# Cross attention: probabilities and keys turned by transposing DMAs in f16 parts, in place of TensorE transposes

## The chip, the cores and the metric

The kernel runs on one core of one Trainium2 chip. The metric is the device time of one execution in microseconds; lower is better. An engine has its own queue of instructions and works in order; engines wait for each other through semaphores. PE is TensorE, DVE is VectorE, ACT is ScalarE, POOL is GpSimd, SP is SyncE, which here only issues DMAs.

## The reference

Two layers on x (128 sequences x 64 positions x 128 channels) and a context of the same shape. The change is in the second layer's cross attention:

```python
x = layer_norm(image_embeds, ln1_g, ln1_b)      # the context
l = layer_norm(latents, ln2_g, ln2_b)           # the running x
q = l @ Wq
kv = concatenate([x, l], axis=1) @ Wkv          # 128 keys per sequence
q, k, v = to_heads(q), to_heads(k), to_heads(v) # 16 heads of 64
w = softmax(einsum('bhqd,bhkd->bhqk', q * scale, k * scale))
out = einsum('bhqk,bhkd->bhqd', w, v)           # heads joined, then @ Wo
```

Before it come an attention by correlation and a quantised feed-forward layer, after it a mixture of 8 experts (two per token). The expert choice of a group of four tiles (normalise, logits, top two, ranks, scatter of the rows to HBM) is computed inside the same block as this attention.

## The kernel before, in words

`build` runs three parts: `load_weights`, `first_layer`, and `attend_and_route`, which calls `cross_attention`, `apply_experts` and `combine`. Only `cross_attention` (from line 901) changes.

The weights are fused ahead: Wq with Wk per head (`qk_fused`), Wv with Wo per head (`vo_fused`), so that each head works on the 128 channels of the normalised rows themselves. Precision is kept by splitting a tensor into a high part in f16 and the rest in f16; `parts_product` (line 110) multiplies two such pairs with three matmuls, on lines 112 to 114, so these lines stand for all split products.

A tile is 128 rows, two sequences; there are 64 tiles, and 4 chunks a tile, 256 in all. A chunk is 8 heads of one sequence. Each engine walks the same steps, from -15 to 298, with one Python function `step` per engine: at step n it does stage S of chunk n + AT_S. The constants on line 976 are thus the schedule, written by hand: a stage with a larger number is done earlier. `number(i, k, off, limit)` gives the chunk and its place, `tile(i, k, off)` the tile in every fourth step, `group` the routing group in every sixteenth. Steps 64 to 239 are a loop of 16 steps, the rest is written out.

The stages of a chunk v, in order:

- tile: SP loads the rows (line 1006 context, 1007 x) to `c_rows`. DVE takes statistics (1113 to 1116), POOL the reciprocal root (1022 to 1026), DVE normalises (1123), POOL applies gain and shift and splits into f16 parts `c_kv_parts` (1030 to 1038). PE transposes the four blocks of parts (1269), and ACT copies them from PSUM to `c_kvT` (1206), of which there are two.
- G (n + 6): PE multiplies the queries' part by the fused weights, ACT writes the high part (1201), DVE the rest (1096).
- S (n + 3): PE makes the scores of 8 heads, 128x512 in PSUM; DVE takes the negated maximum of each row (1081); ACT takes the exponential, four times 128x128 with a running sum (1227), into `c_p`, f32.
- PN (n + 2): DVE inverts the sums (1091), then POOL multiplies `c_p` by them in place (1016).
- PT (n + 0): PE transposes the normalised probabilities, f32, in four matmuls into the bank `PT` (1297); ACT copies the high part to `c_pT..high` (1211), DVE subtracts it from the bank for the rest (1102). There are two such pairs.
- O (n - 1): PE multiplies the turned probabilities by the rows into the one bank `OB` (1303), ACT and DVE split it (1220, 1108).
- W (n - 5): PE sums the 16 heads with the fused weights into `WB`; X3 (n - 9): DVE adds that to x (1077).

Within a step DVE's order is: addition to x, maximum, routing's logits, reciprocal (1091), rest of G (1096), rest of PT (1102), rest of O (1108), statistics, normalising, the rest of routing. ACT's is G, keys, PT, O, exponentials, routing. PE's is keys, G, S, PT, O, W, routing. POOL's is 1016, the roots, the keys' gain and shift, routing, indirect DMAs (1059).

The four buffers of `c_p` are protected by ACT's wait for `pt` (1225); the one bank for turned keys is shared with routing (`KVR`), which is why PE has the waits of `wait_rows` (1247). The waits for the halves of a turned pair are `pt_copied` (1295, 1301).

Of the kernel before, what the change touches and what calls it, by code (L numbers as in the profile page):

```python
# [900 lines left out]
def cross_attention(nc, s, ctx_in, picks, tab, expert):  # L901

    sem = s.sem
    c_loaded = [sem(f"c_ctx_loaded{n}") for n in range(4)]
    names = ("stats rstd kvn kv kvt kvt_copied g g_high g_copied s max exp rden pn pt pt_high pt_copied o o_high o_copied w x3")
# [5 lines left out]
    with ExitStack() as ctx:  # L911
        sb = lambda name, shape, dt=F32: ctx.enter_context(nc.sbuf_tensor(name, shape, dt))
        parts = lambda name, shape: [sb(name + part, shape, F16) for part in ("high", "rest")]
        cs = [sb(f"c_rows{n}", [P, 2, D]) for n in range(4)]
        kv = [sb(f"c_kv{n}", [P, 2, D]) for n in range(4)]
        kvs = [sb(f"c_kv_parts{n}", [P, 2, 2, D], F16) for n in range(4)]
        kvt = [sb(f"c_kvT{n}", [P, 2, 4, 64], F16) for n in range(2)]
        gs = [parts(f"c_g{n}", [P, 2, HEADS1, SEQ]) for n in range(2)]
        pr = [sb(f"c_p{n}", [P, 4, P]) for n in range(4)]
        ptc = [parts(f"c_pT{n}", [P, 4 * P]) for n in range(2)]  # L920
# [38 lines left out]
        PT, OB, KVR, WB = s.pb[4:8]  # L959
        KVB = KVR[:].bitcast(F16)  # L960
# [15 lines left out]
        AT_STATS, AT_RSTD, AT_KVN, AT_KV, AT_KVT, AT_G, AT_S, AT_PN, AT_PT, AT_O, AT_W, AT_X3 = 15, 13, 12, 11, 7, 6, 3, 2, 0, -1, -5, -9  # L976
# [21 lines left out]
        @block.sync  # L998
        def _(sp):
            def step(i, k):  # L1000
                t = 4 * i + k
                if not (known(i) and i == 0):
                    sp.wait_ge(m["kvn"], t - 3)
                for half in range(2):
                    rows = slice(64 * half, 64 * half + 64)
                    sp.dma_start(cs[k][rows, 1 - half, :], cvw[1 - half, t, :, :]).then_inc(c_loaded[k], 16)
                    sp.dma_start(cs[k][rows, half, :], s.xg(i)[rows, k, :]).then_inc(c_loaded[k], 16)
            walk(sp, 0, TILES, 4, 4, TILES, step)
# [63 lines left out]
        def _(dve):  # L1072
            def step(i, k):
# [24 lines left out]
                if n := number(i, k, AT_PT, CHUNKS):  # L1098
                    v, r = n
                    hi, lo = ptc[r % 2]  # L1100
                    dve.wait_ge(m["pt_high"], v + 1)
                    dve.tensor_tensor(lo[:], PT[:], hi[:], ALU.subtract).then_inc(m["pt_copied"], 1)  # L1102
                if n := number(i, k, AT_O, CHUNKS):
# [4 lines left out]
                    dve.tensor_tensor(lo, OB[:].rearrange("p (h c) -> p h c", h=8), hi, ALU.subtract).then_inc(m["o_copied"], 1)  # L1108
                if t := tile(i, k, AT_STATS):
                    v, r, g = t  # L1110
                    dve.wait_ge(c_loaded[r], 64 * (g + 1))
                    for b in range(2):
                        dve.bn_stats(bst[:, b, :], cs[r][:, b, :])
# [3 lines left out]
                if t := tile(i, k, AT_KVN):  # L1117
# [4 lines left out]
                    for n in range(2):  # L1122
                        last = dve.tensor_scalar(kv[r][:, n, :], cs[r][:, n, :], a[:, n, 0:1], b[:, n:n + 1], ALU.subtract, ALU.mult)
# [69 lines left out]
        def _(act):  # L1193
            def step(i, k):
# [7 lines left out]
                if t := tile(i, k, AT_KVT):  # L1202
                    v, r, _ = t
                    act.wait_ge(m["kvt"], v + 1)
                    wait(act, m["s"], 4 * (v - 1))
                    act.activation(kvt[r % 2][:].rearrange("p n a c -> p (n a c)"), KVB[:, 0:512], ACT.Copy).then_inc(m["kvt_copied"], 1)  # L1206
                if n := number(i, k, AT_PT, CHUNKS):
                    v, r = n
                    act.wait_ge(m["pt"], v + 1)
                    wait(act, m["o"], v - 1)  # L1210
                    act.activation(ptc[r % 2][0][:], PT[:], ACT.Copy).then_inc(m["pt_high"], 1)
                if n := number(i, k, AT_O, CHUNKS):
# [5 lines left out]
                    if r % 4 == 1:  # L1218
                        wait(act, m["w"], v - 5)
                    act.activation(os_[r // 4 % 2][0][:, 8 * half:8 * half + 8, 64 * b:64 * b + 64],  # L1220
                                   OB[:].rearrange("p (h c) -> p h c", h=8), ACT.Copy).then_inc(m["o_high"], 1)
# [24 lines left out]
        def _(pe):  # L1246
            def wait_rows(i, k):

                off = AT_KVT - (k + AT_KVT) % 4
                if t := tile(i, k, off):  # L1250
                    pe.wait_ge(m["kvt_copied"], t[0] + 1)

            pe.wait_ge(s.w_moe, 32)

            def step(i, k):
                if t := tile(i, k, AT_KVT):
                    v, r, _ = t
                    pe.wait_ge(m["kv"], v + 1)
                    wait(pe, m["kvt_copied"], v)
                    if (g := group(i, k, ROUTE_TOP + 2)) is not None:  # L1260
                        pe.wait_ge(mr["logits_read"], g + 1)
                    if (g := group(i, k, ROUTE_POS + 2)) is not None:
                        pe.wait_ge(mr["base_read"], g + 1)
                    if (g := group(i, k, ROUTE_XT + 3)) is not None:
                        pe.wait_ge(mr["xt_copied"], g + 1)
                    for part in range(2):
                        for b in range(2):
                            at = 2 * P * part + P * b
# [374 lines left out]
```

## Time and profile before

| | us |
|---|---|
| median of 3 runs | 1600.94 |
| lowest, highest | 1597.19, 1602.82 |
| profiled execution | 1598.53 |
| its span, first to last instruction | 1596.6 |
| PE busy | 1392.2 (87%) |
| DVE busy | 1355.3 (85%) |
| ACT busy | 1280.3 (80%) |
| POOL busy | 1079.0 (68%) |

The first layer ends at about 400 us, the attention with its routing fills the time to about 1270 us, and the experts and the final sum follow. Busy time is the union of the durations of an engine's instructions; these overlap, since an instruction starts before the one before it has ended. "issue" as a releaser is time in which the engine waited for nothing that the profile shows. SPq is the issue of a DMA on SP. The profiled execution's own time is 1.9 us above its span.

### The profile page before, as it was taken

The numbers are of one execution on the slowest core, as the hardware profiler recorded it, in microseconds if no ns is written. First come the engines' busy times: TensorE is split into PE (matmuls) and PEld (weight loads), VectorE is DVE, ScalarE is ACT, GpSimd is POOL, SyncE is SP. The second block draws the span as 40 slices with busy tenths as digits, with TensorE's granted clock in tenths as the row PEclk, the third lists the DMA queues.
The fourth block names the chain that finished last, engine by engine and source line by source line (L and its number), as shares of the span: only waits on it lengthen the run. The fifth ranks groups of instructions, "written<-read, shape, count | busy, mean of one in ns | idle before, by whom it ended". The sixth has DMA issues, their size and how long they took to land. (4 is left out here: it accounts for less than half of the span.)

```text
span 1596.6 us, 53031 instructions
## 1 busy us (share of the span) xinstructions
PE 1392.2 (87%) x17084; PEld 1186.1 (74%) x17084; DVE 1355.3 (85%) x3979; ACT 1280.3 (80%) x3930; POOL 1079.0 (68%) x1524
## 2 busy tenths in 40 slices
PE   4779889974799999999999999999999719999970
PEld 3667777763688888888888888888888618888860
DVE  4479999995799999999999999999999628888877
ACT  1358888875799999999999999999999616666645
POOL 0367877763666577887788778877887555666650
PEclk7989999986899999999999999999999959999995
DMA  5445553400100000000000000000000013332209
GB/s 145 140 158 180 192 202 148 160 2 5 27 13 12 13 20 20 23 22 19 18 22 22 18 18 22 22 18 18 22 15 9 22 43 91 87 84 77 80 28 316
DMA packets 99738, 101.83 MB, mean 64 GB/s; under 512 B 15305, under 2 KB 81132, under 8 KB 99457
## 3 DMA queue, kind: packets, MB, share of 16 engines
q1 hardware_dynamic: 82496, 78.77, 15.4%
q0 software_dynamic: 8640, 16.93, 3.2%
q10 hardware_dynamic: 8448, 4.20, 0.9%
q8 instruction: 83, 1.36, 0.4%
q14 instruction: 71, 0.57, 0.1%
HBM read 39.40 MB, written 57.16 MB: 60 GB/s over the span
## 5 line engine op out<-in xcount | busy, mean ns | idle before, releaser
L1227 ACT ACTIVATE c_p<-bank,c_nmax 128x128 f32<-128x128 f32 x1024 | 368.9, 401 | 2.2 <-DVE c_nmax L1081 1.3
L1016 POOL TENSOR_TENSOR c_p<-c_p,c_rden 128x512 f32<-128x512 f32 x256 | 266.8, 1042 | 110.4 <-DVE c_rden L1091 106.0
L1227 ACT ACTIVATION_READ_ACCUMULATOR c_p<-bank,c_nmax 128x1 f32 x1024 | 244.2, 241 | 0.0
L1403 POOL DMA_INDIRECT moe_outputs<-e_y,e_to x142 | 152.9, 1077 | 93.3 <-DVE e_y L1434 58.6
L112 PE MATMUL bank<-c_kvT,qk_fused 128*128 128x128 f16 x1024 | 185.8, 220 | 10.8 <-ACT c_kvT L1206 10.4
L1081 DVE TENSOR_REDUCE c_nmax<-bank 128x4 f32<-128x512 f32 x256 | 173.4, 677 | 17.5 <-PE bank L114 14.3
L114 PE MATMUL bank<-c_kvT,qk_fused 128*128 128x128 f16 x1024 | 185.7, 220 | 0.0
L113 PE MATMUL bank<-c_kvT,qk_fused 128*128 128x128 f16 x1024 | 185.7, 220 | 0.0
L1473 ACT ACTIVATE e_h<-bank,moe_b 128x256 f32<-128x256 f32 x284 | 117.9, 466 | 65.7 <-PE bank L114 64.4
L1297 PE MATMUL bank<-const,c_p 128*128 128x128 f32 x1024 | 155.9, 275 | 3.6 <-DVE c_pT0rest L1102 1.7
L1059 POOL DMA_INDIRECT moe_slots<-r_rows,r_pos x128 | 131.6, 1028 | 34.9 <-issue 34.9
L112 PEld LDWEIGHTS bank<-c_kvT,qk_fused 128*128 128x128 f16 x1024 | 101.6, 99 | 15.0 <-issue 9.1
L1297 PEld LDWEIGHTS bank<-const,c_p 128*128 128x128 f32 x1024 | 107.7, 141 | 6.8 <-issue 2.4
L113 PEld LDWEIGHTS bank<-c_kvT,qk_fused 128*128 128x128 f16 x1024 | 100.5, 98 | 0.4
L114 PEld LDWEIGHTS bank<-c_kvT,qk_fused 128*128 128x128 f16 x1024 | 100.6, 98 | 0.0
L112 PE MATMUL bank<-vo_fused,c_o1high 128*128 128x128 f16 x512 | 92.2, 219 | 1.4 <-DVE x L1077 1.4
L112 PE MATMUL bank<-vo_fused,c_o0high 128*128 128x128 f16 x512 | 92.5, 219 | 0.5
L112 PE MATMUL bank<-c_kvT,c_g0high 128*128 128x128 f16 x512 | 92.4, 219 | 0.6 <-ACT c_p L1227 0.5
L114 PE MATMUL bank<-c_kvT,c_g1rest 128*128 128x128 f16 x512 | 92.4, 219 | 0.0
L114 PE MATMUL bank<-vo_fused,c_o0rest 128*128 128x128 f16 x512 | 92.4, 219 | 0.0
L113 PE MATMUL bank<-vo_fused,c_o0high 128*128 128x128 f16 x512 | 92.4, 219 | 0.0
L113 PE MATMUL bank<-c_kvT,c_g0high 128*128 128x128 f16 x512 | 92.3, 219 | 0.0
(324 smaller groups left out, 5921.0 us busy)
## 6 DMA issues: line engine op xcount, KB each, us to landing
moe_slots<-slot_fill SPq DMA_DIRECT2D x66, 520.0 KB, 5.6
e_rows<-moe_slots SPq DMA_DIRECT2D x71, 130.0 KB, 2.2
f_z<-moe_outputs SPq DMA_DIRECT2D x32, 256.0 KB, 4.9
x<-in_x SPq DMA_DIRECT2D x16, 256.0 KB, 3.2
a_ctx<-in_ctx SPq DMA_DIRECT2D x32, 128.0 KB, 3.4
moe_stage<-in_L_ffn_W SPq DMA_DIRECT2D x16, 256.0 KB, 3.1
c_rows<-in_ctx SPq DMA_DIRECT2D x128, 32.0 KB, 2.0
c_rows<-x SPq DMA_DIRECT2D x128, 32.0 KB, 1.8
```

The lines of the kernel that those rows point to most:

```text
L112: pe.matmul(out, lhs[0], rhs[0], start=start, stop=False)
L113: pe.matmul(out, lhs[0], rhs[1], start=False, stop=False)
L114: return pe.matmul(out, lhs[1], rhs[0], start=False, stop=stop)
L1016: pool.tensor_tensor(pr[r % 4][:], pr[r % 4][:], rep(rden[r % 4][:], 2, P), ALU.mult).then_inc(m["pn"], 1)
L1059: pool.indirect_dma_start(s.xs, bass.IndirectOffsetOnAxis(ap=pos[:, c, j:j + 1], axis=0), rows[:, j, :], None).then_inc(scattered, 16)
L1081: dve.tensor_reduce(nmax[r % 4][:], SB[r % 2][:].rearrange("p (h c) -> p h c", h=4), AX.X, ALU.max, negate=True).then_inc(m["max"], 1)
L1227: last = act.activation(pr[r % 4][:, h, :], SB[r % 2][:, P * h:P * h + P], ACT.Exp, bias=nmax[r % 4][:, h:h + 1], accum_out=den[r % 4][:, ...
L1297: last = pe.transpose(PT[:, P * h:P * h + P], pr[r % 4][:, h, :], s.ident)
L1403: pool.indirect_dma_start(s.z, bass.IndirectOffsetOnAxis(ap=to[t % YBUF][:, h:h + 1], axis=0), ys[t % YBUF][:, h, :], None, bounds_check=2 ...
L1473: act.activation(hf[t % 2][:, b, :], HB[b][:, 0:TSLOT], ACT.Gelu_apprx_tanh, bias=s.moe_b1[:, bass.ds(e * KB + b, 1)]).then_inc(m["gelu"], 1)
```

## The change

The probabilities are no longer transposed on PE. POOL writes the normalised high part in f16 straight into `c_p_parts` and leaves `c_p` as it is; DVE computes the rest from `c_p`, the reciprocal sums and the high part in four operations, one per 128 columns, a step later (`AT_LOW` = 1). SP turns each part by one transposing DMA of 128x512 f16 into `c_pT`, of which there are now four with both parts. PE's product for O waits for both DMAs by the semaphores `pt_in`. The keys are turned in the same way, one DMA for the four blocks of a tile; `c_kvT` has four buffers. ACT's copies 1206 and 1211, DVE's 1102 and PE's 1269 and 1297 go. The bank that `PT` had becomes a second bank for `OB`, whose parts stay f16 as before. The waits of routing for the shared bank go. SP's walk is written out in full, loads two tiles with four DMAs in place of eight, and in each step issues first the rest of chunk n + 1, then the high part of chunk n + 2, then a tile's keys, then a load.

```diff
-        AT_STATS, AT_RSTD, AT_KVN, AT_KV, AT_KVT, AT_G, AT_S, AT_PN, AT_PT, AT_O, AT_W, AT_X3 = 15, 13, 12, 11, 7, 6, 3, 2, 0, -1, -5, -9
+        AT_STATS, AT_RSTD, AT_KVN, AT_KV, AT_G, AT_S, AT_PN, AT_LOW, AT_O, AT_W, AT_X3 = 15, 13, 12, 11, 6, 3, 2, 1, -1, -5, -9
...
+            def load(n):
+                if n >= 2:
+                    sp.wait_ge(m["kvn"], 2 * n - 2)
                 for half in range(2):
                     rows = slice(64 * half, 64 * half + 64)
...
+            def turn_keys(v):
+                sp.wait_ge(m["kv"], v + 1)
+                if v >= 4:
+                    sp.wait_ge(m["s"], 4 * (v - 3))
+                sp.dma_start_transpose(kvt[v % 4][:].rearrange("p n a c -> p (n a c)").rearrange("p (b c) -> p b c", b=4),
+                                       kvs[v % 4][:].rearrange("p n b d -> p (n b d)")).then_inc(kvt_in[v % 4], 16)
+
+            def turn_weights(v, part):
+                sp.wait_ge(m["p_split" if part else "p_high"], v + 1)
+                if v >= 4 and part == 0:
+                    sp.wait_ge(m["o"], v - 3)
+                sp.dma_start_transpose(ptc[v % 4][:, part, :].rearrange("p (b c) -> p b c", b=4), pp[v % 4][:, part, :]).then_inc(pt_in[v % 4], 16)
+
+            load(0)
+            load(1)
+            for n in range(FIRST, CHUNKS):
+                if 0 <= n + AT_LOW < CHUNKS:
+                    turn_weights(n + AT_LOW, 1)
+                if 0 <= n + AT_PN < CHUNKS:
+                    turn_weights(n + AT_PN, 0)
+                if (n + 9) % 4 == 0 and 0 <= n + 9 < CHUNKS:
+                    turn_keys((n + 9) // 4)
+                if (n + 23) % 8 == 0 and 4 <= (n + 23) // 4 < TILES:
+                    load((n + 23) // 8)
...
                     pool.wait_ge(m["rden"], v + 1)
-                    pool.tensor_tensor(pr[r % 4][:], pr[r % 4][:], rep(rden[r % 4][:], 2, P), ALU.mult).then_inc(m["pn"], 1)
+                    wait(pool, pt_in[r % 4], 32 * (4 * i + (k + AT_PN) // 4))
+                    pool.tensor_tensor(pp[r % 4][:, 0, :].rearrange("p (h c) -> p h c", h=4), pr[r % 4][:], rep(rden[r % 4][:], 2, P),
+                                       ALU.mult).then_inc(m["p_high"], 1)
...
                     dve.reciprocal(rden[r % 4][:], den[r % 4][:]).then_inc(m["rden"], 1)
+                if n := number(i, k, AT_LOW, CHUNKS):
+                    v, r = n
+                    dve.wait_ge(m["p_high"], v + 1)
+                    for h in range(4):
+                        cols = slice(P * h, P * h + P)
+                        last = dve.scalar_tensor_tensor(pp[r % 4][:, 1, cols], pr[r % 4][:, h, :], rden[r % 4][:, h:h + 1], pp[r % 4][:, 0, cols],
+                                                        ALU.mult, ALU.subtract)
+                    last.then_inc(m["p_split"], 1)
...
-                    dve.wait_ge(m["pt_high"], v + 1)
-                    dve.tensor_tensor(lo[:], PT[:], hi[:], ALU.subtract).then_inc(m["pt_copied"], 1)
...
-                    act.activation(kvt[r % 2][:].rearrange("p n a c -> p (n a c)"), KVB[:, 0:512], ACT.Copy).then_inc(m["kvt_copied"], 1)
...
-                    act.activation(ptc[r % 2][0][:], PT[:], ACT.Copy).then_inc(m["pt_high"], 1)
...
                     act.wait_ge(m["max"], v + 1)
-                    wait(act, m["pt"], v - 3)
+                    wait(act, m["p_split"], v - 3)
...
-                            last = pe.transpose(KVB[:, at:at + P], kvs[r][:, part, b, :], s.ident_h[:])
...
-                        last = pe.transpose(PT[:, P * h:P * h + P], pr[r % 4][:, h, :], s.ident)
...
-                    pe.wait_ge(m["pt_copied"], v + 1)
-                    wait(pe, m["o_copied"], v)
+                    pe.wait_ge(pt_in[r % 4], 32 * (4 * i + (k + AT_O) // 4 + 1))
+                    wait(pe, m["o_copied"], v - 1)
```

## Rows read from the trace of the kernel before

**Rows 1.** Busy time by stretch: stretch, its length, PE, PEld, DVE, ACT, POOL, clock, DMA.
```profile
432.47:520.15 87.68, 87.68 (x1220) 77.03 (x1219) 81.78 (x200) 86.77 (x316) 57.41 (x81) 1.00 0.05 13
614.95:1205.24 590.29, 582.39 (x7935) 504.46 (x7933) 560.86 (x1530) 573.15 (x2047) 476.43 (x650) 1.00 0.07 20
```

**Rows 2.** Groups by line on DVE, 614.95 to 1205.24 us: busy, mean ns | idle before.
```profile
L1081 DVE TENSOR_REDUCE c_nmax<-bank 128x4 f32<-128x512 f32 x176 | 119.0, 676 | 7.9 <-PE bank L114 5.5 <-issue 2.5
...
L1123 DVE TENSOR_SCALAR c_kv<-c_rows,c_mv,c_rstd 128x128 f32<-128x128 f32 x88 | 43.2, 531 | 0.0
```

**Rows 3.** Timeline of DVE about 1005 and 1010 us: start, duration, operation.
```profile
1005.08 0.28 DVE L1077 TENSOR_TENSOR x<-x,bank 128x128 f32 x1
1005.27 0.68 DVE L1081 TENSOR_REDUCE c_nmax<-bank 128x4 f32<-128x512 f32 x1
...
1009.95 0.17 DVE L1091 RECIPROCAL c_rden<-c_den 128x4 f32<-128x4 f32 x1
1010.04 0.66 DVE L1096 SCALAR_TENSOR_TENSOR c_g0rest<-bank,c_g0high 128x512 f16<-128x512 f32 x1
1010.61 0.68 DVE L1102 TENSOR_TENSOR c_pT0rest<-bank,c_pT0high 128x512 f16<-128x512 f32 x1
1011.21 0.68 DVE L1108 TENSOR_TENSOR c_o0rest<-bank,c_o0high 128x512 f16<-128x512 f32 x1
```

**Rows 4.** Timeline of ACT, two copies in a row.
```profile
1006.32 0.61 ACT L1206 ACTIVATE c_kvT<-bank 128x512 f16<-128x512 f16 x1
1006.80 0.62 ACT L1211 ACTIVATE c_pT1high<-bank 128x512 f16<-128x512 f32 x1
```

**Rows 5.** Timeline of TensorE's weight loads, the transposes.
```profile
800.17 0.42 PEld L1297 LDWEIGHTS bank<-const,c_p 128*128 128x128 f32 x4
...
801.93 0.27 PEld L1269 LDWEIGHTS bank<-ident_f,c_kv_parts 128*128 128x128 f16 x4
```

**Rows 6.** Line 1565 in the last stage: its group on DVE, and four in the timeline.
```profile
L1565 DVE SCALAR_TENSOR_TENSOR x<-f_z,d_gate,x 128x128 f32<-128x128 f32 x64 | 18.2, 345 | 12.6 <-DMA f_z<-moe_outputs 12.5
...
1572.20 1.14 DVE L1565 SCALAR_TENSOR_TENSOR x<-f_z,d_gate,x 128x128 f32<-128x128 f32 x4
```

**Rows 7.** Groups by line on POOL, 440 to 1230 us.
```profile
L1030 POOL TENSOR_TENSOR c_kv<-c_kv,ln_g 128x256 f32<-128x256 f32 x59 | 42.9, 728 | 0.0
L1033 POOL TENSOR_TENSOR c_kv_parts<-c_kv,ln_b 128x256 f16<-128x256 f32 x59 | 42.9, 726 | 17.0 <-issue 15.4
```

**Rows 8.** Line 545 (least, median, most ns); then SBUF-only DVE operations beside POOL's.
```profile
L545 DVE SCALAR_TENSOR_TENSOR b_qs<-b_qs,b_rr x16: 161/658/1251, 88.3 to 369.3; 128x4 f32<-128x4 f32 x16
L1123 DVE TENSOR_SCALAR c_kv<-c_rows,c_mv,c_rstd x128: 332/340/1829, 400.8 to 1219.0; 128x128 f32<-128x128 f32 x128
...
127.11 1.27 POOL L432 TENSOR_TENSOR x<-x,bit_b 128x512 f32<-128x512 f32 x1
127.74 0.66 DVE L545 SCALAR_TENSOR_TENSOR b_qs<-b_qs,b_rr 128x4 f32<-128x4 f32 x1
...
108.02 1.27 POOL L432 TENSOR_TENSOR x<-x,bit_b 128x512 f32<-128x512 f32 x1
108.09 1.29 DVE L549 TENSOR_SCALAR b_xr<-b_xc,b_qs 128x128 f32<-128x128 f32 x1
```

**Rows 9.** POOL's product behind the reciprocal at 1009.95; waits from 440 to 1230 us.
```profile
1010.20 1.04 POOL L1016 TENSOR_TENSOR c_p<-c_p,c_rden 128x512 f32<-128x512 f32 x1 [0.85 <-DVE c_rden L1091]
...
POOL c_p L1016 <- DVE c_rden L1091: 88.6, 110, 2.3
```

**Rows 10.** A DMA issue on SP; issues by line with KB each, us to landing.
```profile
1005.37 0.49 SPq L1006 DMA_DIRECT2D c_rows<-in_ctx  x1
...
e_rows<-moe_slots SPq DMA_DIRECT2D x71, 130.0 KB, 2.2
f_z<-moe_outputs SPq DMA_DIRECT2D x32, 256.0 KB, 4.9
```

**Rows 11.** Busy time by stretch, end of the first layer.
```profile
340.00:360.00 20.00, 12.62 (x113) 8.92 (x110) 18.44 (x68) 12.68 (x25) 10.98 (x26) 0.74 0.00 1
```

More of the change, by code:

```diff
@@ L903, in cross_attention @@
     sem = s.sem
-    c_loaded = [sem(f"c_ctx_loaded{n}") for n in range(4)]
-    names = ("stats rstd kvn kv kvt kvt_copied g g_high g_copied s max exp rden pn pt pt_high pt_copied o o_high o_copied w x3")
+    c_loaded = [sem(f"c_ctx_loaded{n}") for n in range(2)]
+    kvt_in = [sem(f"c_kvt_in{n}") for n in range(4)]
+    pt_in = [sem(f"c_pt_in{n}") for n in range(4)]
+    names = "stats rstd kvn kv g g_high g_copied s max exp rden p_high p_split o o_high o_copied w x3"
     m = {n: sem("c_" + n) for n in names.split()}
@@ L999, in _ @@
         def _(sp):
[L1000 to L1003, printed above, removed]
+            def load(n):
+                if n >= 2:
+                    sp.wait_ge(m["kvn"], 2 * n - 2)
                 for half in range(2):
                     rows = slice(64 * half, 64 * half + 64)
-                    sp.dma_start(cs[k][rows, 1 - half, :], cvw[1 - half, t, :, :]).then_inc(c_loaded[k], 16)
-                    sp.dma_start(cs[k][rows, half, :], s.xg(i)[rows, k, :]).then_inc(c_loaded[k], 16)
-            walk(sp, 0, TILES, 4, 4, TILES, step)
+                    to = cs[n % 2]
+                    sp.dma_start(to[rows, :, 1 - half, :], cvw[1 - half, 2 * n:2 * n + 2, :, :].rearrange("t s d -> s t d")).then_inc(c_loaded[n % 2], 16)
+                    sp.dma_start(to[rows, :, half, :], s.xg(n // 2)[rows, 2 * (n % 2):2 * (n % 2) + 2, :]).then_inc(c_loaded[n % 2], 16)
+            def turn_keys(v):
[20 more added lines that the diff above has]
+                    load((n + 23) // 8)
         @block.gpsimd
@@ L1122, in step @@
                     for n in range(2):
-                        last = dve.tensor_scalar(kv[r][:, n, :], cs[r][:, n, :], a[:, n, 0:1], b[:, n:n + 1], ALU.subtract, ALU.mult)
+                        last = dve.tensor_scalar(kv[r][:, n, :], cs[r // 2][:, r % 2, n, :], a[:, n, 0:1], b[:, n:n + 1], ALU.subtract, ALU.mult)
                     last.then_inc(m["kvn"], 1)
@@ L1246, in _ @@
         def _(pe):
[L1247 to L1251, printed above, removed]
             pe.wait_ge(s.w_moe, 32)
             def step(i, k):
[L1256 to L1268, printed above, removed]
-                            last = pe.transpose(KVB[:, at:at + P], kvs[r][:, part, b, :], s.ident_h[:])
-                    last.then_inc(m["kvt"], 1)
                 if n := number(i, k, AT_G, CHUNKS):
                     v, r = n
-                    t = r // 4 % 2
-                    if r % 4 == 0:
-                        pe.wait_ge(m["kvt_copied"], 4 * i + (k + AT_G) // 4 + 1)
+                    t = r // 4
+                    if u := tile(i, k, AT_G):
+                        pe.wait_ge(kvt_in[u[1]], 16 * (u[2] + 1))
                     wait(pe, m["g_copied"], v - 1)
@@ L1283, in step @@
                     v, r = n
-                    half, b, t = r % 2, r // 2 % 2, r // 4 % 2
+                    half, b, t = r % 2, r // 2 % 2, r // 4
                     pe.wait_ge(m["g_copied"], v + 2 if r % 4 == 0 else v - r % 4 + 4)
@@ L1288, in step @@
                         at = 8 * half + 2 * h
[L1289 removed]
+                        last = parts_product(pe, SB[r % 2][:, P * h:P * h + P], [part[:, b, at:at + 2, :] for part in gs[t % 2]],
                                              [kvt[t][:, part, 2 * b:2 * b + 2, :] for part in range(2)])
                     last.then_inc(m["s"], 1)
[L1292 to L1298 removed]
                 if n := number(i, k, AT_O, CHUNKS):
                     v, r = n
[L1301 to L1303 removed]
+                    pe.wait_ge(pt_in[r % 4], 32 * (4 * i + (k + AT_O) // 4 + 1))
+                    wait(pe, m["o_copied"], v - 1)
+                    parts_product(pe, OB[r % 2][:], [kvs[r // 4][:, part, r // 2 % 2, :] for part in range(2)],
+                                  [ptc[r % 4][:, part, :] for part in range(2)]).then_inc(m["o"], 1)
                 if n := number(i, k, AT_W, CHUNKS):
```

41 lines of the change are left out of this document (10 added, 31 removed).

## The prediction

> **What bounds the kernel now.** I read the page first. The attention block keeps PE, DVE and ACT busy at once, so the end of the chain of waits (it ends in the last stage) says nothing about it, and no single wait does. So I took the busy time by stretch [rows 1]. From 614.95 to 1205.24 us, 176 chunks (the reduction of line 1081 runs once a chunk [rows 2]), the period is 590.29/176 = 3.354 us. Of that PE is busy 3.31, ACT 3.26, DVE 560.86/176 = 3.187 and POOL 2.71 us. The first three are within 5% of each other: a gain needs all three lighter, a loss only one heavier. Before the routing joins in, the period is 87.68 us for 28 chunks, 3.13 us [rows 1].
>
> Durations overlap on an engine, so I price by the distance from one start to the next, in the timeline. On DVE [rows 3] a 128x512 operation takes 0.60 us of the queue, a reciprocal 0.09, the addition of 128x128 without a scalar operand 0.19 (1005.08 to 1005.27). On ACT a 128x512 copy takes 0.48 us [rows 4]. On PE the weight loads of the four f32 transposes take 0.42 us, those of the four f16 transposes of the keys 0.27 [rows 5].
>
> **The change, part by part, per chunk.**
> PE loses the four transposes of the probabilities, 0.42, and a quarter of those of the keys, 0.07. Its 3.31 becomes 2.82. The second bank for the output only loosens a wait.
> ACT loses the high part of the turned probabilities, 0.48, and a quarter of the key copy, 0.12: 3.26 becomes 2.66.
> DVE loses the rest part of line 1102, 0.60. It gains four operations of 128x128 with a scalar from SBUF and two tensors in SBUF. The same form stands in the last stage, line 1565: four in 1.14 us, 0.345 one, so (1.14 - 0.345)/3 = 0.265 from start to start, 1.06 for four [rows 6]. 3.187 - 0.60 + 1.06 = 3.65 us. That alone is past the present period.
> POOL keeps its 1.04 us product and writes f16 instead (1033, f16 out, and 1030, f32 out, take 726 and 728 ns [rows 7]: nothing).
>
> **The port.** The four new DVE operations read only SBUF; the one removed read PSUM. The trace shows what SBUF-only operations meet beside a POOL tensor operation. A scalar_tensor_tensor of 128x4 with two SBUF tensors, 0.161 us at best, took 0.66 at 127.74 and ended 0.02 after the POOL product begun at 127.11 [rows 8]. In a run of four back-to-back operations at line 549, POOL's product started at 108.02, between them, and the third, started at 108.09, took 1.29 [rows 8]: DVE doesn't keep its place through a run. Line 1123 takes 332 ns at best and 531 in the mean [rows 2, 8]; its worst, 1.83, is long enough for two POOL operations in a row. After the change the collision is built in: POOL waits for the reciprocal of its chunk and starts 0.25 us after that starts (1009.95 to 1010.20 [rows 3, 9]), and the new operations stand directly behind it in DVE's queue. It waits so now 110 times in the 790 us from 440 to 1230, before about every second product [rows 9]; with a longer period it will before nearly all. The first new operation starts at 0.09 and the second at 0.35; POOL takes the gap at about 0.3 and holds to 1.34. An operation so held ends some 0.1 to 0.17 after POOL's, against 0.70 unhindered: 0.8 us lost, and I add 0.04 for POOL's other tensor operations. Bounds: 0 (DVE keeps its run) and 1.5 (1.83 - 0.33, two losses). I take 0.84, since the row nearest in form and place loses to just one. DVE: 3.65 + 0.84 = 4.49 us.
>
> **The queue of SP.** It now carries, per chunk, two transposing DMAs of 128 KB, a quarter of one for the keys, and 0.5 loads in place of 1: 2.75 DMAs. The issue of a plain one takes 0.49 us [rows 10], so 1.4 us, no bound. What a transposing DMA costs is in no row. Below: the issue alone, 0.5. Above: if each held the queue as long as the 256 KB loads take to land, 4.9 us; the nearest in size, 130 KB, lands in 2.2 [rows 10]. Transfers don't hold the issue of the next ones in any row, so I take under 1.9, which is where 2.25 x T + 0.25 reaches 4.5. Latency is covered: the rest part is written early in step n and PE wants it late in step n+2, over 4.5 us, against 2.2; the high part is issued a step earlier. In the queue, behind the wait for POOL's high part stand the next rest part, the keys and the loads; the keys have three steps and the loads eight, so these cost nothing. If that cover is gone, PE stands behind its new wait, but has 4.49 - 2.82 = 1.7 us to spare. ACT's new wait is for a split made a step earlier, POOL's for DMAs of four chunks ago: both free.
> Two pages of the Trainium skill speak on this. "VectorE: DVE Perf Modes", The three transpose paths, gives 1309 ns for a DMA transpose of 128x128 against 390 on TensorE; the estimate from it, four blocks one after another, is 5.2 us a DMA and 11.8 us a chunk, some 3750 us in all. "Advanced Engine Details and Errata", X-Bar Transpose, says such DMAs are as fast as plain ones, an estimate of 0.4 us for 128 KB, and my sum stands. No row here decides between them.
>
> **The sum.** 4.49 - 3.354 = 1.136 us x 256 chunks = 291 us, on the profiled execution's 1598.53: 1889. The median of the runs is 2.4 us higher, so I say 1891. In the stretch without routing both terms drop by about the same. Filling and emptying the pipeline changes by a few DMA latencies.
>
> **The rivals.**
> (a) DVE keeps its run or POOL comes late: 3.65 us, +0.30 x 256 = +76, 1677; with half the collisions, 1784. For: POOL's 2.71 us of work often makes it late now. Against: line 549, and the longer period. Chance 0.21 up to 1800.
> (b) The queue is the bound. If a transposing DMA holds it as long as the 130 KB load takes to land [rows 10], T = 2.2 us, the period is 2.25 x 2.2 + 0.25 = 5.2, +1.85 x 256 = +473, 2073; T = 2.5 gives 2250, T = 4.9 gives 3630. It decides from T = 1.9 on. For: four blocks of 128 columns, a form no row has. Against: plain issues cost 0.5. Chance 0.20. (The transpose-path page of the skill is on its side.)
> (c) The clock. With PE busy 2.82 of 4.49 us its granted clock may fall: it was 0.74 where PE was busy 12.62 of 20 us [rows 11], 1.00 in the block [rows 1]. At the lower of the two levels (1.2 of 2.4 GHz) the work is 5.6 us a chunk, 2180 at most, and a PE so busy gets its clock back. Against: its gaps are under 2 us. Chance 0.04.
> (d) Faster: the split is cheap on DVE. This needs four operations that each take less than (3.354 - 3.187 + 0.60)/4 = 0.19 us of the queue with no port loss, the cost of the addition without a scalar. Then 3.187 - 0.60 + 0.76 less the 0.08 that line 1123 now loses to POOL is 3.27, -0.08 x 256 = -21, 1580. Against: the scalar form's own row and the port rows. Chance 0.06; between it and (a) nothing changes, 0.04.
> My forecast, DVE with the port at 4.15 to 5.0 us, 1800 to 2020, has 0.45.
>
> **The numbers.** About 0.3% is what a measurement of this kernel can tell from no change. Faster 0.06, same 0.04, slower 0.90. The range runs from (a), 1660, to T = 2.5 in (b), 2250; below lie 0.10, above 0.08. The likeliest case's own range is 1800 to 2020.
>
> **What would show it.** DVE near 100% busy in the block, at 4.5 us a chunk; the new DVE operations in two kinds, 0.35 and over 1 us, the long ones ending just after POOL's product; PE and ACT waiting on DVE. Wrong if all four take 0.35 (rival a), if SP's queue has no gap and PE waits for the turned probabilities (b), if the clock is under 1 in the block (c), or if the period is under 3.35 us.

## The result, and the profile after

The changed kernel takes 1934.11 us (median of 4 runs, 1927.42 to 1935.23) against 1600.88 for the kernel before; the ratio is 1.2076, 95% interval 1.2041 to 1.2111. It is slower, and nearly all of the rise lies in the attention block. The measure of that block used from here on is the distance from the first to the last maximum of the scores on DVE, 255 periods. The two rows are those of the maximum in each kernel, before and after (line, form, least/median/most ns, first to last start):

```profile
L1081 DVE TENSOR_REDUCE c_nmax<-bank x256: 655/680/693, 411.7 to 1255.3; 128x4 f32<-128x512 f32 x128
```

```profile
L1110 DVE TENSOR_REDUCE c_nmax<-bank x256: 655/676/693, 413.7 to 1586.9; 128x4 f32<-128x512 f32 x128
```

The block grew from 843.6 to 1173.2 us, by 329.6 of the 333; the mean period from 3.31 to 4.60 us. Inside the block, busy time by stretch, changed kernel (columns as in [rows 1]):

```profile
600.00:1200.00 600.00, 448.47 (x5128) 365.89 (x5128) 584.88 (x1496) 346.86 (x1328) 361.23 (x471) 0.83 0.39 78
```

DVE is busy 97.5% of it, in 128 chunks: 4.57 of 4.69 us a chunk. ACT has fallen from 97% to 58%, POOL from 81% to 60%, PE from 99% to 75%, its granted clock from 1.00 to 0.83. Where DVE's time goes, groups by line in that stretch (busy, mean ns | idle before), answering to [rows 2]:

```profile
L1126 DVE SCALAR_TENSOR_TENSOR c_p_parts<-c_p,c_rden,c_p_parts 128x128 f16<-128x128 f32 x512 | 276.1, 598 | 0.0
L1110 DVE TENSOR_REDUCE c_nmax<-bank 128x4 f32<-128x512 f32 x128 | 86.9, 679 | 7.0 <-PE bank L114 5.5
...
L1155 DVE TENSOR_SCALAR c_kv<-c_rows,c_mv,c_rstd 128x128 f32<-128x128 f32 x64 | 18.9, 334 | 0.0
```

The four new operations keep DVE 276.1/128 = 2.16 us a chunk. The row of line 1565 [rows 6] has 1.14 for four alone. Line 1155 (1123 before) has gone from 531 to 334 ns in the mean, 2 ns above its least [rows 8]: it hardly meets POOL any more. The timeline of one group (start, us, engine, line, operation), DVE first, then POOL. The view merges operations that follow each other, so three windows of growing length give the group's first operation alone (x1), the first two (x2) and all four (x4). It answers to [rows 8, 9]:

```profile
1001.26 0.17 DVE L1120 RECIPROCAL c_rden<-c_den 128x4 f32<-128x4 f32 x1
1001.34 0.32 DVE L1126 SCALAR_TENSOR_TENSOR c_p_parts<-c_p,c_rden,c_p_parts 128x128 f16<-128x128 f32 x1
1001.34 1.43 DVE L1126 SCALAR_TENSOR_TENSOR c_p_parts<-c_p,c_rden,c_p_parts 128x128 f16<-128x128 f32 x2
1001.34 2.43 DVE L1126 SCALAR_TENSOR_TENSOR c_p_parts<-c_p,c_rden,c_p_parts 128x128 f16<-128x128 f32 x4
...
1001.59 1.04 POOL L1044 TENSOR_TENSOR c_p_parts<-c_p,c_rden 128x512 f16<-128x512 f32 x1 [2.51 <-DVE c_rden L1120]
1002.59 0.78 POOL L1065 TENSOR_TENSOR c_kv<-c_kv,ln_b 128x256 f32<-128x256 f32 x1
```

The collision is the one drawn in the prediction: the first operation takes 0.32 us, POOL starts 0.33 after the reciprocal's start, the second ends at 1002.77, some 0.14 behind the product. Here the group then meets POOL's operation for the rows' shift as well. The next group meets the product, but no such operation:

```profile
1006.14 1.90 DVE L1126 SCALAR_TENSOR_TENSOR c_p_parts<-c_p,c_rden,c_p_parts 128x128 f16<-128x128 f32 x4
...
1006.29 1.06 POOL L1044 TENSOR_TENSOR c_p_parts<-c_p,c_rden 128x512 f16<-128x512 f32 x1 [1.99 <-DVE c_rden L1120]
1007.32 0.24 POOL L1051 TENSOR_TENSOR c_rstd<-c_mv,c_norm_mul 128x2 f32<-128x2 f32 x1
```

All 128 groups of the stretch, sorted by what POOL runs beside them, are of these two kinds: every one meets the product; 64 also meet a per-tile operation of 128x256 and take 2.38 us in the mean, the other 64 take 1.93. Who waits for whom in the changed kernel, 600 to 1500 us (us in total, times, longest):

```profile
POOL c_p_parts L1044 <- DVE c_rden L1120: 290.3, 167, 3.3
ACT c_p L1249 <- DVE c_nmax L1110: 165.5, 119, 2.5
...
PE bank L112 <- DVE x L1106: 133.9, 48, 3.2
...
PE bank L112 <- DMA c_pT<-c_p_parts: 23.1, 36, 2.3
```

The long waits are for DVE; PE's waits for the transposing DMAs are 23 of 900 us. SP's queue waits for DVE too, 600 to 1200 us:

```profile
SPq L1023 <- DVE c_p_parts L1126: 182.1, 104, 2.8
```

What the prediction had no row for, the transposing DMA on SP's queue (least, median and most ns of the issue, and us to landing):

```profile
L1023 SPq DMA_TRANSPOSE c_pT<-c_p_parts x512: 1188/1216/2230, 417.8 to 1595.7; - x171
...
DMA to landing us min/median/max: 2.4/2.5/4.4
```

### The profile page after: what moved, and what is told of

It is laid out like the page before. It is cut to its first block and busy times, and to the rows that moved or that the text cites. A ratio compares the mean times of both kernels' runs of the same rounds, so it can differ in the third digit from the quotient of the medians.

```text
span 1932.1 us, 50785 instructions
## 1 busy us (share of the span) xinstructions
PE 1430.2 (74%) x15788; PEld 1174.9 (61%) x15804; DVE 1707.3 (88%) x4747; ACT 1139.8 (59%) x3610; POOL 1108.7 (57%) x1524
## 3 DMA queue, kind: packets, MB, share of 16 engines
q8 instruction: 79, 1.29, 0.3%
## 5 line engine op out<-in xcount | busy, mean ns | idle before, releaser
L1126 DVE SCALAR_TENSOR_TENSOR c_p_parts<-c_p,c_rden,c_p_parts 128x128 f16<-128x128 f32 x1024 | 547.0, 592 | 0.0
L1044 POOL TENSOR_TENSOR c_p_parts<-c_p,c_rden 128x512 f16<-128x512 f32 x256 | 273.0, 1066 | 412.5 <-DVE c_rden L1120 411.8
L112 PE MATMUL bank<-c_kvT,qk_fused 128*128 128x128 f16 x1024 | 215.3, 240 | 35.9 <-DMA c_kvT<-c_kv_parts 17.9
L113 PE MATMUL bank<-c_kvT,qk_fused 128*128 128x128 f16 x1024 | 214.3, 240 | 0.0
L114 PE MATMUL bank<-c_kvT,qk_fused 128*128 128x128 f16 x1024 | 213.6, 239 | 0.0
L1242 ACT ACTIVATE c_o1high<-bank 128x512 f16<-128x512 f32 x128 | 77.2, 603 | 136.0 <-PE bank L114 136.0
L1242 ACT ACTIVATE c_o0high<-bank 128x512 f16<-128x512 f32 x128 | 76.9, 601 | 110.7 <-PE bank L114 110.5
L112 PEld LDWEIGHTS bank<-c_kvT,qk_fused 128*128 128x128 f16 x1024 | 113.1, 110 | 47.0 <-DVE c_g0rest L1133 16.3
L112 PE MATMUL bank<-c_kvT,c_g0high 128*128 128x128 f16 x512 | 106.1, 238 | 43.6 <-DVE c_g0rest L1133 43.6
L112 PE MATMUL bank<-c_pT,c_kv_parts 128*128 128x512 f16 x256 | 110.3, 431 | 37.0 <-DMA c_pT<-c_p_parts 36.9
L112 PE MATMUL bank<-c_kvT,c_g1high 128*128 128x128 f16 x512 | 102.6, 233 | 45.7 <-DVE c_g1rest L1133 45.7
L112 PEld LDWEIGHTS bank<-vo_fused,c_o0high 128*128 128x128 f16 x512 | 57.4, 112 | 108.8 <-DVE x L1106 92.4
```

What stands on the lines that cost most here:

```text
L112: pe.matmul(out, lhs[0], rhs[0], start=start, stop=False)
L113: pe.matmul(out, lhs[0], rhs[1], start=False, stop=False)
L114: return pe.matmul(out, lhs[1], rhs[0], start=False, stop=stop)
L1044: pool.tensor_tensor(pp[r % 4][:, 0, :].rearrange("p (h c) -> p h c", h=4), pr[r % 4][:], rep(rden[r % 4][:], 2, P), ALU.mult).then_inc(m[ ...
L1126: last = dve.scalar_tensor_tensor(pp[r % 4][:, 1, cols], pr[r % 4][:, h, :], rden[r % 4][:, h:h + 1], pp[r % 4][:, 0, cols], ALU.mult, ALU ...
```

## The experiments

The runs were made on three chips: e1 to e4, e5 to e8, and e9 to e11. The kernel before took 1664.85 us beside e1 to e4 and 1600.16 and 1600.45 beside the others. The excess is outside the block (the experts' first and last product are 287 us apart in e3_keys_only, 228 in the kernel before), so I compare blocks, and totals only as ratios to the kernel before on the same chip. A block is read from one profiled execution of each kernel; e4 and e8, the same kernel on two chips, differ in it by 0.4 us. The kernel before itself spread from 1646 to 1677 us beside e1 to e4, so the ratios of e1 and e4 are known only to 0.8%.

**e1_rest_first.** The port against the form: the block of the four operations stands ahead of the maximum instead of behind the reciprocal.

```diff
+                if n := number(i, k, AT_LOW, CHUNKS):
+                    ...
                 if n := number(i, k, AT_S, CHUNKS):
...
-                if n := number(i, k, AT_LOW, CHUNKS):
-                    ...
```

> The changed kernel with one thing moved: within a step DVE computes the rest of chunk n+1 before the maximum and the reciprocal instead of behind the reciprocal, so the four SBUF-only operations no longer stand where POOL's product is let go. Nothing is left out. Theory (DVE is the bound, and of its 4.6 us a chunk about 1.0 is time in which the four operations wait for POOL): the four operations fall from 2.1 us of the queue towards 1.06, some collisions with POOL's per-tile and routing operations stay (0.2 to 0.4), the period goes from 4.69 to 3.9, and the time to about 1735 us (1690 to 1790). Rival (the four operations are simply slow in this form, 0.5 us each, wherever they stand): no change, 1915 to 1950. Rival (SP's queue, 1.22 us for each transposing DMA, is the true bound): its 2.25 x 1.22 + 0.25 = 3.0 us a chunk would have to be full, and nothing would change either.

Ratio 1.097 (1.0899 to 1.1041), against 1.2076. The maximum's row in this kernel (line, form, least/median/most ns, first to last start):

```profile
L1118 DVE TENSOR_REDUCE c_nmax<-bank x256: 673/678/692, 412.6 to 1417.3; 128x4 f32<-128x512 f32 x128
```

The group's row, 600 to 1200 us (busy, mean ns | idle before):

```profile
L1112 DVE SCALAR_TENSOR_TENSOR c_p_parts<-c_p,c_rden,c_p_parts 128x128 f16<-128x128 f32 x592 | 207.9, 410 | 4.9 <-issue 1.9 <-POOL c_p_parts L1044 1.6
```

The block is 1004.7 us, a period of 3.94 where 3.9 was expected; the group costs 207.9/148 = 1.40 us instead of 2.16. The same operations with the same data, only placed elsewhere in the step: half of the loss goes. It would be a little more if the normalising of line 1155 did not meet POOL again, at 630 ns in place of 334:

```profile
L1155 DVE TENSOR_SCALAR c_kv<-c_rows,c_mv,c_rstd 128x128 f32<-128x128 f32 x74 | 43.7, 630 | 0.6 <-POOL c_rstd L1055 0.6
```

The rival, that the four are slow wherever they stand, is out. The total, 1824.25 us, lies above the range I gave, but that was for a chip on which the kernel before takes 1600.9; 1.097 x 1600.9 would be 1756, within it.

**e2_no_rest.** What is next if DVE is free.

```diff
-                    for h in range(4):
-                        ...
-                    last.then_inc(m["p_split"], 1)
+                    dve.nop().then_inc(m["p_split"], 1)
```

> The changed kernel without the four DVE operations that compute the rest of the probabilities: the rest parts are zeroed once, and the semaphore is raised by an empty instruction; both DMAs still run. So the probabilities have only their high part. Theory (DVE is the bound): DVE falls to 2.5 us a chunk, and the next are SP's queue at 3.0, POOL at 2.9 and PE at 2.8; period 3.0 to 3.2, time 1510 to 1560 us, below the kernel before. Rival (queue or latency of the transposing DMAs set the period, DVE only waits beside it): the time stays above 1800 us. Port theory alone can't be told apart here from the cost of the operations themselves; e1_rest_first does that.

This was a miss in size. Ratio 1.0066 (1.0028 to 1.0105); the block is 852.9 us, 3.345 a chunk, not 3.0 to 3.2. The rival, above 1800 us, is out: with the four operations gone 320 us of block go. DVE is free, as the theory wants, and yet nothing is gained on the kernel before. The maximum's row:

```profile
L1110 DVE TENSOR_REDUCE c_nmax<-bank x256: 656/691/693, 412.2 to 1265.1; 128x4 f32<-128x512 f32 x128
```

Busy time of 600 to 1200 us (columns as in [rows 1]):

```profile
600.00:1200.00 600.00, 516.66 (x7168) 434.32 (x7166) 489.58 (x1374) 476.07 (x1859) 484.72 (x661) 0.98 0.54 109
```

The timeline of SP's queue, and PE's weight loads a little later:

```profile
1000.38 0.61 SPq L1009 DMA_DIRECT2D c_rows<-in_ctx  x1
1001.05 0.62 SPq L1010 DMA_DIRECT2D c_rows<-x  x1
1001.71 0.61 SPq L1009 DMA_DIRECT2D c_rows<-in_ctx  x1
1002.36 0.61 SPq L1010 DMA_DIRECT2D c_rows<-x  x1
1003.02 1.28 SPq L1023 DMA_TRANSPOSE c_pT<-c_p_parts  x1
...
1006.44 0.10 PEld L112 LDWEIGHTS bank<-c_pT,c_kv_parts 128*128 128x128 f16 x1 [2.78 <-DMA c_pT<-c_p_parts]
```

No engine is above 87%. SP's queue runs nearly without a gap: transposes follow each other at 1.26 to 1.35 us, four loads in a row hold them up for 2.6 us, and PE's weight loads then stand for 2.78. A chunk issues two transposes of the probabilities, a quarter of one of the keys' and half a load: 2.25 x 1.28 + 0.5 x 0.66 is 3.2 us, of 3.345 measured. Summed over the trace from 600 to 1200 us, the issues fill 563 of the 600 us (396 in the changed kernel). So the queue looks full, a reading which e7 tests. The expectation had it at 3.0 us, from the issue's duration instead of the distance between starts.

**e3_keys_only.** The kernel before with one part of the change, the keys by DMA.

```diff
+                sp.dma_start_transpose(kvt[v % 4]..., kvs[v % 4]...).then_inc(kvt_in[v % 4], 16)
-                            last = pe.transpose(KVB[:, at:at + P], kvs[r][:, part, b, :], s.ident_h[:])
-                    act.activation(kvt[r % 2]..., KVB[:, 0:512], ACT.Copy).then_inc(m["kvt_copied"], 1)
```

> The kernel before with only the keys turned by a transposing DMA (one of 128x512 f16 a tile, four buffers of turned keys), probabilities as before on TensorE. Nothing is left out. It takes 0.07 us a chunk off PE and 0.12 off ACT, and nothing off DVE. Theory (three engines within 5% of each other share the bound, so relief of two gives a part of it): period 3.354 to about 3.30, 1580 to 1593 us. Rival (DVE at 3.19 with its collisions is as much the bound as PE): 1596 to 1604 us, no change. If the DMA's latency were a wait: above 1604.

Ratio 1.0039 (1.0001 to 1.0077), block 844.9 against 843.6: no gain, the rival was right. 0.07 us off PE and 0.12 off ACT are worth nothing here; that DVE's 3.2 is the reason is an argument, not shown by this run alone.

**e4_more_matmuls** and **e8_more_matmuls_again**. What the clock costs. e4 ran on the other chip and was repeated beside e5.

```diff
                     for h in range(4 * (r % 4), 4 * (r % 4) + 4):
+                        for _ in range(2 if h % 4 else 0):
+                            pe.matmul(WB[:, P:4 * P], s.vo[:, 0, 0, :], s.vo[:, 0, 0:3, :], start=False, stop=False)
```

> The changed kernel with six more f16 matmuls of 128x384 a chunk on TensorE, written to unused columns of the output bank, about 1 us of PE a chunk; all results are computed as before. They are there to hold the granted clock, which is 0.83 between 600 and 1200 us in the changed kernel. Theory (DVE sets the period, the clock costs nothing): clock to 0.95 or more, time unchanged within 15 us of 1934. Rival (the slower clock lengthens the chain from PE's product to DVE's maximum and carries 30 us or more): 1900 us or less. If PE had become the bound, the time would rise by up to 1 us a chunk, 2190 us.

> The same as e4_more_matmuls, beside the changed kernel on one chip. There the block was 1157.5 us at a granted clock of 0.97, 16 us under the changed kernel's 1173 at 0.83 on another chip. If the clock carries these 16 us: 10 to 25 us under e5_changed_again. If it was the chip: within 5 us of it.

**e5_changed_again**, the changed kernel without an edit, on e8's chip.

> The changed kernel itself, unedited, on the chip of the runs beside it, as their yardstick. Its block, from the first to the last maximum of the scores on DVE, took 1173 us (255 periods of 4.60) against 844 before. If a chip differs from another only outside the block (DMA-heavy stages), the block is 1165 to 1180 here too, whatever the total.

e5: 1931.87 us, block 413.2 to 1583.1, 1169.9 us. e8: 1919.08 us, 1157.1. e4: ratio 1.1925, block 1157.5, so blocks agree across chips. Busy time of 600 to 1200 us, e5 and then e8:

```profile
600.00:1200.00 600.00, 442.33 (x5153) 360.81 (x5152) 586.50 (x1502) 349.00 (x1338) 363.83 (x473) 0.85 0.39 78
```

```profile
600.00:1200.00 600.00, 511.15 (x5989) 396.34 (x5988) 590.11 (x1516) 359.22 (x1348) 368.21 (x478) 0.97 0.39 79
```

The edit adds six matmuls of 128x384 to PE's work in each chunk, and the kernel is 12.8 us faster, all in the block: the granted clock rises from 0.85 to 0.97 and DVE's share from 97.8 to 98.4%. So the clock costs some 13 us here, of 330, with the added work already taken off. A part of it is DVE's wait for PE's scores before the maximum, 4.3 of 600 us in e5 and 1.2 in e8. The expectation of e8 held (10 to 25 us). That of e4 just failed: its clock rose to 0.97 as expected, but I had allowed 15 us, and the block is 15.7 under the changed kernel's 1173.2; by its ratio it would be 1909 us on the first chip, 25 under, give or take 12. The blocks, the better measure, are also short of the rival's 30 us.

**e6_no_product.** The port by itself.

```diff
-                    pool.tensor_tensor(pp[r % 4][:, 0, :].rearrange("p (h c) -> p h c", h=4), pr[r % 4][:], rep(rden[r % 4][:], 2, P),
-                                       ALU.mult).then_inc(m["p_high"], 1)
+                    pool.nop().then_inc(m["p_high"], 1)
```

> The changed kernel without POOL's product: the high parts are zeroed once and POOL raises the semaphore by an empty instruction; the four DVE operations, all DMAs and all waits stay. So the probabilities have no high part. Port theory: without its partner the group of four falls from 2.1 us of DVE's queue to 1.06, most of them 0.34 us long, the period from 4.60 to about 3.65 (3.6 to 3.85 with what POOL's per-tile operations still cost), the block to 920 to 980 us, total 190 to 250 us under the changed kernel's on the same chip. Rival (form, not port): the group stays at 2 us and the block above 1120.

1717.56 us, ratio 1.0744 (1.0716 to 1.0771), 214 us under e5; block 962.7, period 3.78: all as expected. The maximum's row, and then the group's in 600 to 1200 us:

```profile
L1109 DVE TENSOR_REDUCE c_nmax<-bank x256: 655/678/692, 411.3 to 1374.0; 128x4 f32<-128x512 f32 x128
```

```profile
L1125 DVE SCALAR_TENSOR_TENSOR c_p_parts<-c_p,c_rden,c_p_parts 128x128 f16<-128x128 f32 x626 | 210.6, 396 | 0.0
```

Per chunk the group costs 210.6/156 = 1.35 us. Of the changed kernel's 2.16, then, 0.81 are waits for this one product, 1.14 the operations themselves [rows 6], and 0.21 are left for waits for POOL's other operations, which are still there. The groups of this run, sorted in the same way as above, bear that out: the 78 that meet no POOL operation of 128x256 take 1.11 us in the mean, the other 78 take 1.58. By these numbers the operations alone are 1.11, the product adds 1.93 - 1.11 = 0.82, and the per-tile operations 0.45 to 0.47 in every second group, 0.23 a chunk.

**e7_no_rest_dma.** SP's queue as the next bound: e2_no_rest without the rest's DMA; POOL and PE wait for one DMA a chunk in place of two.

```diff
-                if 0 <= n + AT_LOW < CHUNKS:
-                    turn_weights(n + AT_LOW, 1)
```

> Kernel e2_no_rest (no rest operations on DVE) with also the DMA of the rest part left out, its turned parts zeroed once: one transposing DMA a chunk in place of two. e2_no_rest had a block of 853 us, a period of 3.345, with DVE only 82% busy. Theory (behind DVE the queue of SP is the next bound: transposing DMAs follow each other at 1.26 to 1.35 us, 2.25 of them and four loads of 0.65 every eighth chunk are 3.2 us a chunk, and a burst of loads makes PE wait 2.8 us): the period falls to 3.0 to 3.15, POOL's and PE's work, the block to 765 to 805 us, PE no longer waits for turned probabilities. Rival (latency from POOL over the DMA to PE, or POOL itself, set the 3.345): block stays at 840 or more.

1534.47 us, ratio 0.9581 (0.956 to 0.9602); block 779.8, period 3.06. As expected. The maximum's row:

```profile
L1108 DVE TENSOR_REDUCE c_nmax<-bank x256: 656/683/692, 415.3 to 1195.1; 128x4 f32<-128x512 f32 x128
```

The wait of SP's queue, 600 to 1200 us:

```profile
SPq L1023 <- POOL c_p_parts L1042: 248.0, 159, 3.2
```

Busy time of the same stretch:

```profile
600.00:1200.00 600.00, 545.68 (x7640) 454.24 (x7640) 508.52 (x1459) 509.54 (x1985) 508.99 (x693) 1.00 0.35 73
```

SP now waits 248 us for POOL, and its issues fill only 341 of the 600 us, against 563 in e2; PE is busy 91%, and its waits for the turned probabilities are 1.7 us in the whole execution, against 79.1 in e2. So the queue did bound e2. The kernel leaves out the rest part of the probabilities, so it is no substitute for either kernel. At 191 maxima in the stretch, PE's work is 545.68/191 = 2.86 us a chunk and ACT's 2.67: the prediction's 2.82 and 2.66 for the lightened engines fit.

**e9_before_no_rest.** The same part left out of the kernel before.

```diff
-                    dve.tensor_tensor(lo[:], PT[:], hi[:], ALU.subtract).then_inc(m["pt_copied"], 1)
+                    dve.nop().then_inc(m["pt_copied"], 1)
```

> The kernel before without the operation of DVE that makes the rest of the turned probabilities (line 1102); the rest is zeroed once, the semaphore raised by an empty instruction, all matmuls stay. It is the partner of e7_no_rest_dma, which leaves the same part out of the changed kernel and had a period of 3.06 us and 1534 us. It asks what the turning by DMA is worth when nobody pays for the split. Theory (three engines share the bound; without 0.60 us on DVE, PE at 3.31 and ACT at 3.26 still hold the period): block 825 to 844 us, total 1582 to 1601, so the turning by DMA is worth 45 to 65 us of its own. Rival (DVE alone was the bound of the kernel before): block under 805, and the DMA's own worth is small.

1588.71 us, ratio 0.9925 (0.9907 to 0.9943), block 414.9 to 1246.3, 831.4 us. Taking 0.60 us off DVE gives 12 us; PE (592 of 600 us busy) and ACT (588) hold the rest, as expected. Against e7 the difference is 51.6 us of block: this is what turning by DMA is worth, with the second output bank that comes with it, when the split is free and one DMA is enough.

**e10_one_operation.** Another split, nothing left out.

```diff
-                    pool.tensor_tensor(pp[r % 4][:, 0, :]..., pr[r % 4][:], rep(rden[r % 4][:], 2, P), ALU.mult).then_inc(m["p_high"], 1)
+                    pool.tensor_tensor(pr[r % 4][:], pr[r % 4][:], rep(rden[r % 4][:], 2, P), ALU.mult).then_inc(m["pn"], 1)
...
+                    act.activation(pp[r % 4][:, 0, :], pr[r % 4][:].rearrange("p h c -> p (h c)"), ACT.Copy).then_inc(m["p_high"], 1)
...
+                    dve.tensor_tensor(pp[r % 4][:, 1, :], pr[r % 4][:].rearrange("p h c -> p (h c)"), pp[r % 4][:, 0, :],
+                                      ALU.subtract).then_inc(m["p_split"], 1)
```

> The changed kernel with another split: POOL normalises in place in f32 as before the change, ACT copies the high part from SBUF (0.48 us), and DVE makes the rest in one subtraction of 128x512, placed behind the rest of the output; both DMAs are issued a step later for the high part. Nothing is left out. DVE 3.19 - 0.60 + 0.60 = 3.2 us, a few collisions with POOL's per-tile operations more, ACT 3.14, PE 2.82, SP's queue 3.2. Theory (form and place of the split are what the changed kernel pays for): period 3.3 to 3.6, block 840 to 920, total 1597 to 1680, level with the kernel before at best, since two resources sit at 3.2. Rival (an SBUF-only operation of 128x512 loses to POOL as often and as long as the four): period above 3.9. Rival (the later high part makes PE wait for the DMAs): period above 3.6 with PE's waits on the turned probabilities over 100 us of 600.

1703.4 us, ratio 1.0635 (1.0609 to 1.0661); block 417.0 to 1365.8, 948.8, period 3.72: above my range (3.3 to 3.6), and neither rival as stated (above 3.9; PE's waits over 100 us). The operation's group on DVE, 600 to 1200 us:

```profile
L1133 DVE TENSOR_TENSOR c_p_parts<-c_p,c_p_parts 128x512 f16<-128x512 f32 x162 | 176.2, 1087 | 0.0
```

PE's wait in the same stretch:

```profile
PE bank L112 <- DMA c_pT<-c_p_parts: 72.2, 59, 2.9
```

One meeting with POOL, in the timeline:

```profile
1002.30 0.67 DVE L1133 TENSOR_TENSOR c_p_parts<-c_p,c_p_parts 128x512 f16<-128x512 f32 x1
...
1002.29 1.27 POOL L1056 TENSOR_TENSOR c_kv<-c_kv,ln_g 128x256 f32<-128x256 f32 x1
```

One operation takes 1.09 us in the mean against 0.67 undisturbed, so the port still costs 0.42 a chunk; and in this meeting, where DVE was not held, POOL is the loser, 1.27 us for what takes 0.73 [rows 7]. Both engines pay. How much of the period PE's 72 us of waits for the DMAs add was not separated. This is the best whole kernel with turned probabilities that I ran, and it doesn't reach the kernel before.

**e11_rest_last.** The four operations behind the rest of the output.

```diff
-                if n := number(i, k, AT_LOW, CHUNKS):
-                    ...
                 if n := number(i, k, AT_G, CHUNKS):
...
                     dve.tensor_tensor(lo, OB[r % 2][:].rearrange("p (h c) -> p h c", h=8), hi, ALU.subtract).then_inc(m["o_copied"], 1)
+                if n := number(i, k, AT_LOW, CHUNKS):
+                    ...
```

> The changed kernel with the four operations behind the rest of the output on DVE, 1.3 us after the reciprocal, when POOL's product ought to be over. Nothing is left out. e1_rest_first, which put them ahead of the maximum, had a block of 1005 us. Port theory: the same or a little better or worse by which of POOL's per-tile operations they now meet, block 960 to 1040, total 1715 to 1800. Rival (in e1 it was the order ahead of the maximum that helped, not the partner at the port): block above 1120.

1807.56 us, ratio 1.1293 (1.1269 to 1.1317), block 415.6 to 1465.3, 1049.7, a period of 4.12: just above both ranges, far below the rival's. The group's row, 600 to 1200 us:

```profile
L1138 DVE SCALAR_TENSOR_TENSOR c_p_parts<-c_p,c_rden,c_p_parts 128x128 f16<-128x128 f32 x570 | 248.2, 494 | 0.0
```

PE's wait in the same stretch:

```profile
PE bank L112 <- DMA c_pT<-c_p_parts: 119.7, 75, 2.9
```

The timeline of two steps, DVE then POOL:

```profile
1000.60 1.13 DVE L1138 SCALAR_TENSOR_TENSOR c_p_parts<-c_p,c_rden,c_p_parts 128x128 f16<-128x128 f32 x4
...
1002.90 0.17 DVE L1120 RECIPROCAL c_rden<-c_den 128x4 f32<-128x4 f32 x1
...
1004.16 1.92 DVE L1138 SCALAR_TENSOR_TENSOR c_p_parts<-c_p,c_rden,c_p_parts 128x128 f16<-128x128 f32 x4
...
999.60 1.03 POOL L1044 TENSOR_TENSOR c_p_parts<-c_p,c_rden 128x512 f16<-128x512 f32 x1 [1.04 <-DVE c_rden L1120]
...
1002.79 1.01 POOL L1073 TENSOR_TENSOR r_rstd<-r_rstd,minus_half 128x4 f32<-128x4 f32 x1
1003.94 0.20 POOL L1075 TENSOR_TENSOR r_shift<-r_shift,r_rstd 128x4 f32<-128x4 f32 x1
1004.10 1.04 POOL L1044 TENSOR_TENSOR c_p_parts<-c_p,c_rden 128x512 f16<-128x512 f32 x1
```

The group costs 248.2/142 = 1.75 us. In the first step the product is over as the group begins, and the four take 1.13 us. In the second POOL was late, held up by routing: its product starts 1.20 us behind the reciprocal and meets the operations after all. Placing them a fixed distance behind the reciprocal helped only where POOL had been waiting for it. The later rest also makes PE wait 120 us for the DMA.

## Why the prediction was right

The forecast was 1891 us, slower, by the port; it is 1934. The range and the likeliest case's own range hold it.

- **What bounds.** DVE was named as the engine that a heavier load would make the bound. It is 97.5% busy from 600 to 1200 us; PE, ACT and POOL wait for it, and e2 shows that without the four operations the block is 320 us shorter. Shown.
- **The form.** 1.06 us of DVE's queue from line 1565's row. No run has the group without all of POOL's operations, but the traces hold single groups that meet none of any length: 1.13 us in e11, 1.11 in the mean of 78 in e6, from the first start to the last end, of which the next operation overlaps 0.08 (in the changed kernel the group at 1006.14 ends at 1008.04 and line 1133 starts at 1007.96). That is 1.03 to 1.05 of the queue. Shown.
- **The product at the port.** 0.80 predicted from the distance of starts; 0.81 by e6 against the changed kernel. e1 agrees in another way: with the same operations and the product kept, but placed apart, the group costs 1.40. Shown, twice. The condition that was argued, that with a longer period POOL would wait for nearly every reciprocal, came true as well: it waits 111 times in 128 chunks.
- **POOL's other operations.** This term of the sum was mis-sized: 0.04 us, measured 0.21 to 0.23. The prediction let a group lose to just one POOL operation; every second group loses to two. I had looked at the one operation tied to the reciprocal and hardly at the per-tile ones directly behind it (1059 to 1067 in the changed kernel), which take the port next, as at 1002.59. Against this, 0.10 came back from line 1123, which I had left as it was: (531 - 334) ns, at half an operation a chunk. That the two errors are of opposite sign is luck.
- **The clock.** I gave the lower clock as a rival with a chance of 0.04, for the case that PE becomes the bound, and against it said that PE's gaps would be under 2 us. The gaps were up to 3.2 us, the clock did fall, to 0.83 at PE 75% busy, and PE did not become the bound; by e8 it costs 13 us. A rival that happens in part belongs into the sum.
- Together: in the stretch from 600 to 1200 us the period is 4.69 where 4.49 was forecast. DVE's work is 4.57 of it: 3.187 - 0.60 + 2.16 for the group - 0.08 of overlap - 0.10 for line 1123. The other 0.12 is idle time, which the forecast had at nothing. Over the block the rise is 1.29 us a chunk against 1.136, 330 us against 291.
- **SP's queue.** I took T under 1.9 us from a plain issue of 0.49; it is 1.22. No bound in the changed kernel, right, though only by 4.6 against 3.2. The page "VectorE: DVE Perf Modes" of the Trainium skill, The three transpose paths, gives 1309 ns for one block of 128x128; four blocks in one DMA land in 2.5 us, so my estimate of 5.2 from it, block after block, doesn't hold. The other page of the Trainium skill that the prediction named, "Advanced Engine Details and Errata", X-Bar Transpose (TRN2), has transposing DMAs as fast as regular ones: near enough for the landing, 2.5 us against 2.2 for a plain one of 130 KB [rows 10], but not for the issue, 1.22 against 0.49.
- **What was costed at nothing** stayed so or nearly: POOL's f16 output (1066 ns in the mean against 1043 before; the port may be the difference, which isn't shown), the keys' DMA (e3), and ACT's and POOL's new waits, which don't appear among the waits.

What stays open: whether a loop of the waits adds the last 0.07 us of the 0.12 idle a chunk, beside the clock's 0.05, and whether another order of POOL's work could keep all its operations off DVE's; neither was tried.

## What to carry to other kernels

Before moving an elementwise operation to where both of its tensors lie in SBUF, look at what POOL is doing at that moment, and price the operation by a row of the same form beside a POOL tensor operation, not by its duration alone. Here one event, the reciprocal, released POOL just as the SBUF-only operations of DVE began, and they met in every one of 128 groups; look for such an event, and also at what POOL does next. And when three engines are level, ask of each edit which of the three gets heavier: taking work off PE and ACT bought nothing here (e3, and e2 with DVE's share gone too, where a fourth queue was full at once), while the form and the port on DVE made the block 330 us longer.

## What I had not expected of the hardware

A transposing DMA of 128x512 f16 takes SP's queue for 1.19 to 1.22 us at each issue, 2.4 times a plain load's 0.49 and twice the 0.61 of the changed kernel's larger loads; with two and a quarter a chunk and half a load the queue was full at a period of 3.345 us (e2, e7). PE's granted clock fell to 0.83 at 75% busy, with waits of at most 3.2 us (3.7 before its weight loads); six matmuls a chunk whose results nobody uses brought it to 0.97 and made the kernel 13 us faster (e8). And POOL can lose at the port as well as DVE (1.27 us in place of 0.73, e10).
